# Turning a half's maxima with one VectorE transpose and a DRAM table in a fused attention and expert kernel

## The reference

```python
xn = _layernorm(x)
# attention, 16 heads of dk = 8
ctx = xn @ We.T
influence = einsum('bqe,bke->bqk', ctx, ctx)
scores = einsum('bhqd,bhkd->bhqk', Q, K) / sqrt(dk) + 0.1 * influence[:, None]
attn = softmax(scores, axis=-1)
att = einsum('bhqk,bhkd->bhqd', attn, V).reshape(b, s, d) @ Wo.T
# experts: 8 of them, two per token
probs = softmax(xn @ gate_w.T); topk_probs, topk_idx = top_k(probs, 2)
y = (gelu(x @ w1[e] + b1[e]) @ w2[e] + b2[e]) for the two chosen experts
out = x + att + sum(y * topk_probs)
```

## Time and profile before

| | us |
|---|---|
| median of 3 runs (710.57 to 712.48) | 710.75 |
| the profiled execution | 710.7 |
| its span in the trace | 708.9 |
| PE busy | 645.0 (91%) |
| DVE busy | 613.8 (87%) |
| ACT busy | 540.8 (76%) |
| POOL busy | 469.0 (66%) |

### The profile page before, as it was taken

One profiled execution on the slowest core, in us unless ns is written; L12 is line 12 of the kernel. 1 busy time (PEld: TensorE's weight loads), 2 busy tenths in 40 slices (PEclk: granted clock), 3 DMA queues, 4 the chain that ended last, 5 costly groups with the idle time before them and its releaser, 6 DMA issues.

```text
span 708.9 us, 22900 instructions
## 1 busy us (share of the span) xinstructions
PE 645.0 (91%) x7800; PEld 431.6 (61%) x7800; DVE 613.8 (87%) x1106; ACT 540.8 (76%) x1123; POOL 469.0 (66%) x542
## 2 busy tenths in 40 slices
PE   0367899999999999879999999999999999999996
PEld 0254445555555555569999999999455555555553
DVE  8979899999899899758888888887999999999991
ACT  2583478888888888758888888888787887778785
POOL 8680478687677657125566566566688888878883
PEclk9996799999999999999999999999999999999999
DMA  9859566676686776564444454543576877788742
GB/s 249 305 161 338 150 160 180 179 204 167 178 199 178 184 183 172 148 109 100 101 106 102 101 96 110 103 99 79 142 169 174 191 186 187 175 189 195 179 112 76
DMA packets 162975, 113.71 MB, mean 160 GB/s; under 512 B 72624, under 2 KB 150448, under 8 KB 162864
## 3 DMA queue, kind: packets, MB, share of 16 engines
q1 hardware_dynamic: 153632, 90.63, 51.5%
q0 software_dynamic: 8192, 16.86, 9.8%
q10 hardware_dynamic: 1040, 4.76, 1.8%
HBM read 55.42 MB, written 47.19 MB: 145 GB/s over the span
## 4 chain that ended last, share of the span: by engine, by line
PE 62%; DVE 16%; SPq 9%; DMA 7%; issue 4%; ACT 1%; DVEq 0%; ACTq 0%
PE bank L1243 14%; PE mx L1232 13%; PE bank L1125 12%; PE bank L1103 10%; DVE mx L948 8%; PE mx L1137 6%; DMA stack<-qk_dram 4%; PE bank L1023 2%; PE bank L1185 2%; DVE A L783 2%; SPq L322 2%; DVE lo_qk L966 2%; DMA stack<-mT 2%; SPq L326 1%; PE bank L1154 1%
## 5 line engine op out<-in xcount | busy, mean ns | idle before, releaser
L700 ACT ACTIVATE A<-bank 128x512 f32<-128x512 f32 x502 | 278.0, 597 | 57.6 <-PE bank L1125 48.7
L948 DVE TENSOR_REDUCE mx<-mx 128x4 f16<-128x1024 f32 x256 | 302.5, 1205 | 18.4 <-PE mx L1137 15.9
L571 POOL TENSOR_SCALAR rows<-rows,slot_p 128x128 f32<-128x128 f32 x142 | 112.2, 800 | 99.0 <-DVE rows L999 99.0
L1125 PE MATMUL bank<-stack 113*128 113x256 f16 x1004 | 170.1, 276 | 1.8 <-ACT A L700 0.8
L557 POOL DMA_INDIRECT slots_x<-rows,pos x128 | 124.0, 969 | 50.9 <-PE bank L1125 30.0
L601 POOL DMA_INDIRECT rows<-slots_y,pos x128 | 122.0, 953 | 37.1 <-issue 18.2
L1103 PE MATMUL bank<-A,V 128*32 128x256 f32 x2048 | 137.1, 385 | 1.8 <-ACT A L700 1.7
L744 ACT ACTIVATE rows<-mx,b 128x256 f32<-128x256 f32 x284 | 111.5, 475 | 30.2 <-PE mx L1232 29.9
L1125 PEld LDWEIGHTS bank<-stack 113*128 113x128 f16 x1004 | 73.2, 97 | 89.6 <-ACT A L700 48.7
L993 DVE TENSOR_TENSOR rows<-rows 128x512 f16<-128x512 f32 x142 | 101.2, 714 | 24.5 <-ACT rows L748 22.1
L1243 PE MATMUL bank<-w,rows 128*128 x1704 | 108.4, 220 | 4.4 <-DVE rows L993 4.4
(11 more groups left out here) (142 smaller groups left out, 591.4 us busy)
## 6 DMA issues: line engine op xcount, KB each, us to landing
stack<-ctx_rest SPq DMA_DIRECT2D x64, 256.0 KB
stack<-qk_dram SPq DMA_DIRECT2D x128, 96.0 KB
slots_y<-rows SPq DMA_DIRECT2D x71, 128.0 KB, 2.1
qk_dram<-hi_qk SPq DMA_DIRECT2D x64, 128.0 KB
stack<-ctx_high SPq DMA_DIRECT2D x128, 64.0 KB
slots_x<-A ACTq DMA_DIRECT2D x1, 4644.0 KB, 19.8
w_stage<-in_w SPq DMA_DIRECT2D x8, 512.0 KB
qk_dram<-lo_qk SPq DMA_DIRECT2D x64, 64.0 KB
```

Source lines behind the costliest of these rows:

```text
L571: ins = pool.tensor_scalar(ye[n % 4][:, h, :], ye[n % 4][:, h, :], slot_p[:, n // 4 % 3, n % 4, h:h + 1], None, ALU.mult)
L700: act.activation(A[:, n % NA, :, :].rearrange("p h s -> p (h s)"), scores(k, n)[:, :], ACT.Exp, scale=SCALE).then_inc(s_xp, 1)
L948: dve.tensor_reduce(mx[:, a, 8 * qt:8 * qt + 8].rearrange("q (i e w) -> q i e w", i=2, e=2)[:, :, g % 2], MX[u % 2][:, :].rearrange("q (i ...
L1125: mm = pe.matmul(scores(k, n)[:, i * S:(i + 1) * S], stack[0:SHIFT + 1, par, h, 1, c * P:(c + 1) * P], stack[0:SHIFT + 1, par, h, 0, :], s ...
```

## The change

The maxima go to the shift row by another way. `mx` gets another order of columns, so that one column holds one head and one half of the queries (`f`), with `f` innermost. One `transpose` over 128 partitions turns the four 32 x 32 blocks each in its place: row 32j + 2h + f of `mT` then holds queries 32j to 32j + 31 of half `f`, for head `h`. `shift_out` writes them, in two DMAs of 32 pieces of 64 bytes, into a new table in DRAM, `shift_dram`, head by head and query by query. `shift_in` waits until both have landed (semaphore `s_mw`), and reads the table back into the shift row with one DMA.

```diff
+        shift_dram = nc.dram_tensor("shift_dram", [2, H, S], F16, kind="Internal").ap()
...
-        mT = sb("mT", [32, 2, 2, P], F16)
+        mT = sb("mT", [P, 2, 2, 32], F16)
...
-            def shift_rows(a, b1_, par1):
-
-                sp.wait_ge(s_mt, 2 * b1_ + a + 1)
+            def shift_out(a, b, par):
+
+                sp.wait_ge(s_mt, 2 * b + a + 1)
                 for c in range(2):
-                    sp.dma_start(stack[SHIFT:SHIFT + 1, par1, 8 * a:8 * a + 8, 0, c * P:(c + 1) * P], mT[8 * c:8 * c + 8, par1, a, :]).then_inc(s_mr[par1][a], 16)
+                    blocks = shift_dram[par, 8 * a:8 * a + 8].rearrange("h (c j q) -> c j h q", c=2, q=32)[c]
+                    sp.dma_start(blocks, mT[c:P:4, par, a, :]).then_inc(s_mw[par][a], 16)
+
+            def shift_in(a, b, par, half):
+
+                sp.wait_ge(s_mw[par][a], 32 * (half + 1))
+                sp.dma_start(stack[SHIFT:SHIFT + 1, par, 8 * a:8 * a + 8, 0, :], shift_dram[par, 8 * a:8 * a + 8]).then_inc(s_mr[par][a], 16)
...
+                if attention_flags(k - 1, 0 if first_half else HALF)["m"]:
+                    shift_in(1, b, par, half)
...
                     if f["m"]:
-                        shift_rows(g, b1_, par1)
+                        shift_out(g, b1_, par1)
...
                         write(par3, n_hq, n_lq)
+                    if g == 0 and f["m"]:
+                        shift_in(0, b1_, par1, s.at(1)[2])
...
-                            for i in range(4):
-                                ins = dve.transpose(mT[:, par1, a, 32 * i:32 * i + 32], mx[32 * i:32 * i + 32, a, :])
-                            ins.then_inc(s_mt, 1)
+                            dve.transpose(mT[:, par1, a, :], mx[:, a, :]).then_inc(s_mt, 1)
```

More of the change, by code:

```diff
@@ L255, in build @@
         s_mr = [[sem(f"s_mr{i}_{a}") for a in range(2)] for i in range(2)]
+        s_mw = [[sem(f"s_mw{i}_{a}") for a in range(2)] for i in range(2)]
         s_mx, s_red, s_mt = (sem(n) for n in ("s_mx", "s_red", "s_mt"))
@@ L947, in attend @@
                         dve.wait_ge(s_mx, 8 * b1_ + u + 1)
-                        dve.tensor_reduce(mx[:, a, 8 * qt:8 * qt + 8].rearrange("q (i e w) -> q i e w", i=2, e=2)[:, :, g % 2], MX[u % 2][:, :].rearrange("q (i w k) -> q i w k", i=2, w=2), AX.X, ALU.max).then_inc(s_red, 1)
+                        dve.tensor_reduce(mx[:, a, :].rearrange("q (i e w f) -> q i e w f", i=2, e=2, w=2)[:, :, g % 2, :, qt], MX[u % 2][:, :].rearrange("q (i w k) -> q i w k", i=2, w=2), AX.X, ALU.max).then_inc(s_red, 1)
                         if u in (3, 7):
@@ L951, in attend @@
                             if k is None or b1_ >= 2:
-                                dve.wait_ge(s_mr[par1][a], 32 * half1)
-                            for i in range(4):
-                                ins = dve.transpose(mT[:, par1, a, 32 * i:32 * i + 32], mx[32 * i:32 * i + 32, a, :])
-                            ins.then_inc(s_mt, 1)
+                                dve.wait_ge(s_mr[par1][a], 16 * half1)
+                            dve.transpose(mT[:, par1, a, :], mx[:, a, :]).then_inc(s_mt, 1)
                     if u == 0 and f["c"]:
@@ L1116, in shifted @@
                         if p == 0 and u in (0, 4):
-                            pe.wait_ge(s_mr[par][u // 4], 32 * (half + 1))
+                            pe.wait_ge(s_mr[par][u // 4], 16 * (half + 1))
                         back = len(ring) if k == B - 1 and n >= 2 else 2
```

## The result

The changed kernel takes 756.9 us (median of 4 runs, 749.5 to 761.1) against 711.2 for the kernel before: a ratio of 1.061, interval 1.051 to 1.070. In a second series, on another chip and beside three experiments, it was 755.3 us, ratio 1.060, interval 1.056 to 1.064. Medians and ranges hold every execution; the ratios and intervals leave out those more than 1.5% above the fastest of their kernel. The kernel before spreads over 0.3% in the first series and the changed one over 1.5%; the granted clock of PE goes with a part of that spread (E4 and E6).

A forecast was written before the change was run, and what follows sets the result against it. It saw PE and DVE almost full in attention, and a loop through load 0, shift row and shifted products with 0.7 us slack. 31 x (1.7 - 0.4) = 40 us on 710.7 gave 750, range 718 to 800.

The forecast's parts named there:

- the likeliest case: In attention, half 0's shift row lands late and PE stalls in each step: 750 us, range 725 to 778, chance 0.60.
- the stall: PE in unit 0 stands still for half 0's shift row: 1.7 us in 31 sequences, bounds 0.7 and 4.2.
- what comes back: After each stall PE meets fewer waits for ACT and DVE: 0.4 us per sequence, bounds 0 and 1.26 per half.
- DVE's turn: Four turns of 0.20 us become one of 0.20, giving DVE back 0.64 per half, 41 us in 64 halves.
- one turn costs as much as four: Rival: DVE gets nothing back and the return is perhaps 0.2 us per step: 757 us; no chance of its own.
- The hops: DMA to and from DRAM: the first lands in 3.3 us, the second in 2.4, so the row lands at 216.6.
- Half 1: Its row lands at 223.4, PE wants it by 223.9 at most: hidden behind half 0's stall, or costing tenths.
- The signs to look for: Profile after: PE waits about 1 to 2 us in some 30 places, always unit 0; step about 14.8, not 13.5.
- faster by DVE's relief: Rival: DVE was the bound and the hop is hidden: 679 to 711 us, 700 with a third; chance 0.06.
- A hidden hop: Rival: the hop is hidden or nearly, DVE's relief worth nothing: 709 to 720 us, about 713; chance 0.12.
- Heavy hops: Rival: small pieces and queued writes slow both hops in most steps, half 1 stalls too: 788, up to 829; chance 0.22.

The follow-up runs named there:

- E4: The changed kernel with eight idle products on PE in unit 0 ahead of the wait for the shift row: 749.7 us, ratio 1.053.
- E6: The changed kernel with four idle products on PE ahead of the wait for half 0's shift row: 747.6 us, ratio 1.050.
- E1: The kernel before with one turn over 128 partitions, its shift copies reading a tile of zeros, without a second hop: 711.2 us, ratio 0.999.
- E5: The changed kernel with the turn done in four instructions on 32 partitions each: 752.3 us, ratio 1.052.
- E9: The kernel before, with its four turns, in which only half 1's row goes through the table in DRAM: 730.6 us, ratio 1.028.
- E10: The kernel before, with its four turns, in which only half 0's row goes through the table in DRAM: 747.4 us, ratio 1.045.
- E3: The changed kernel with shift_in reading another finished table in DRAM, so without waiting for the first hop: 748.2 us, ratio 1.051.
- E7: The changed kernel with half 0's shift_in issued by ACT behind unit 6's exponentials, not by SP: 761.2 us, ratio 1.065.
- E2: The changed kernel with shift_in of half 0 ahead of the four writes in SP's list: 792.2 us, ratio 1.111.
- E8: The changed kernel with shift_in reading another finished table, right behind the load and ahead of shift_out in both halves: 712.2 us, ratio 0.999.

## Why the prediction held, step by step

It said 750 us, 718 to 800, with 0.88 on slower. The measured 757 and 755 lie in it, and the likeliest case was the mechanism: SP's place and the first hop make the row late for unit 0, and PE waits for it in nearly every sequence. That the number came out so near is in part luck: the stall and what comes back were both taken too large, and the clock was left out.

- *DVE's turn*: taken at 0.20, measured 0.211 on 128 partitions, so the rival by which one turn costs as much as four falls. The Trainium skill, "VectorE: DVE Perf Modes", section "The three transpose paths", gives 0.311 for a 128 x 128 turn in bf16; the 0.211 here does not exceed it. DVE's busy time fell from 613.8 to 582.3 us, 31.5 and not 41: 256 turns of 0.200 are 51 us and 64 of 0.211 are 13.5, so 38 went there; I had counted the gaps as well. The reductions, costed at nothing, grew by 3 us, and what makes up the other 3 is not shown.
- *The hops* were mis-sized: "I take 3.3" for the first was 2.80 in the quiet step, "2.4" for the second 1.96, and an issue of `shift_out` takes 0.53, not 0.64. There the row lands 7.52 us after the load and not 8.6, and the stall is 0.84, not 1.7. Over all steps the stalls in unit 0 have a median of 1.1 us, and with the longest their sum is 41.5 us, 1.3 per sequence. The Trainium skill, "DMA: Bandwidth & Descriptors", section "Latency and other measured facts", has about 0.8 us as the least for a tiny transfer. No hop on the chain of the changed kernel comes near it: the shortest took 1.88.
- *What comes back*, taken at 0.4 per sequence, is the term that was most over-sized. The quiet step seems to bear it out (6.59 to 6.26), but 6.59 belongs to the longer kind of step before; the ordinary one has 6.32, so 0.06 came back. Over the span PE waited 44.0 us for the row and its idle time grew by 41.3: 2.7 us, some 0.1 per sequence. DVE's relief has no part in it, as E1 and E5 show, and the weight loads' waits for ACT grew (48.7 to 54.1).
- *The missing term* is the granted clock. The sum had none; the step from 229.76 shows 1.6 us for one fall, and the slower products sum to 8.5 us, 0.3 per sequence. So in place of 1.7 - 0.4 = 1.3 per sequence the profile has 44.0 / 31 = 1.4 of stall, less 0.1 that comes back, with 0.3 of slower products: 1.6.
- *Half 1* "just hides behind the stall of half 0", "and if not, it costs tenths": right in the main for PE's waits (2.4 us in the changed kernel against 16.0 in E9, where half 1 is alone and costs 20 us). But the changed kernel is 11 us above E10, 0.35 per sequence, so the sum should have had those tenths.
- *The signs to look for*: line 364 does start near behind line 339 (243.16 against an end of 242.88), which I had called a sign against; the chain shows that the first hop landed at 243.15 all the same. Both arrive together, and E3, E7 and E2 show that taking one away does not help. Seven of the 37 waits stand in unit 4, another sign against, but they hold only 2.4 of 44.0 us. The step was to be 14.8 in place of 13.5: over the 29 steps its mean is 14.9 in place of 13.2.
- *The rivals*: faster by DVE's relief is refuted by E1 (its bound of 32.1 us counted stalls twice; 26.2 is the most that the rows allow), a cost of the transfers as such by E8. A hidden hop is refuted by the waits for the row. Heavy hops occur, in some steps.

What makes a hop long in one step and not in another was not settled.

## What to carry to other kernels

A transfer that hardly anybody waits for may still have less than a microsecond to spare, some 0.7 us by the prediction's estimate here: count from the event that allows it to be issued to the instruction that needs it, and compare with one round trip, before splitting it in two. Savings on DVE, which looked 92% busy, were worth nothing here, where its relief did not shorten the step; take the work away in an experiment, leaving everything else, before trading latency for it. And a queue that waits in the middle delays what stands behind: a wait is best put where other issues already cover it, as E2 shows against the changed kernel. And one step is not the kernel: a term read from a single step is best read from several, since this kernel has two kinds.

## What the runs showed of the hardware that I had not expected

- A stall of 1.86 us in otherwise full work was followed by a stretch at a granted clock of 0.50, after one of 0.84 the groups of products were as quick as before. The length of the stall alone does not tell: in the same profile the clock stayed at 1.00 behind one of 1.93 us (at 115.95), and fell to 0.50 behind one of 1.19 (at 582.20), which had another gap of 0.57 shortly ahead of it. With four idle products in the gap (E6) the granted clock of the attention stretches was 0.99 in place of 0.96 and 0.97.
- An issue on SP took 0.53 us for 32 pieces of 64 bytes into DRAM; the pair with 8 pieces of 256 bytes each (E9) took 0.63 in all, and one with a single partition as its goal 0.65.
